# Layer 1 attention on TensorE: sixteen units written out instead of a loop, and another order of the work in front of the first step

## The reference

```python
q, k, v = (proj(wq), proj(wk), proj(wv))
q, k = apply_rope(q, k, sin, cos)
att = jnp.einsum('bhqd,bhkd->bhqk', q, k) * (1.0 / math.sqrt(HD))
att = jax.nn.softmax(att, axis=-1)
y = jnp.einsum('bhqk,bhkd->bhqd', att, v)
```

## Time and profile before

| | us |
|---|---|
| median of 3 runs | 3000.16 (2997.89 to 3001.02) |
| the profiled execution | 2999.55 |
| its span, first to last instruction | 2997.8 |
| first projection of layer 1 attention on PE | 1177.80 |
| first scores of unit 0 | 1244.63 |
| first copy of y (tick 2, step 0) | 1289.28 |
| last copy of y (tick 17, step 8) | 2402.01 |

### The profile page before, as it was taken

The page is one execution under the profiler, slowest core; times in us unless marked ns, Lnnn a source line. Parts: engine busy times, 40 slices in busy tenths (PEclk is TensorE's granted clock), DMA queues, the critical chain, the costliest instruction groups (busy, mean ns, idle before and its releaser), DMA issues. The chain is left out here.

```text
span 2997.8 us, 54358 instructions
## 1 busy us (share of the span) xinstructions
PE 2848.9 (95%) x19392; PEld 2011.7 (67%) x19392; DVE 1857.0 (62%) x2721; ACT 1291.0 (43%) x2021; POOL 1416.7 (47%) x1003
## 2 busy tenths in 40 slices
PE   6999999799999997799999999999999789999999
PEld 5878787688888886455555555555555368888887
DVE  5656766577777764666666666666666744444444
ACT  3221111266666663355555555555555522222222
POOL 2003555122333222377777777777777732222222
PEclk9999999999999998799999999999999999999999
DMA  3221211122232224122222222222222332222221
GB/s 127 88 61 49 65 61 53 36 71 85 84 105 84 84 90 160 58 71 71 71 71 72 71 71 71 71 71 71 72 78 77 121 127 85 85 89 86 91 84 49
DMA packets 124567, 238.99 MB, mean 80 GB/s; under 512 B 13440, under 2 KB 48384, under 8 KB 124416
## 3 DMA queue, kind: packets, MB, share of 16 engines
q1 hardware_dynamic: 120896, 235.32, 23.2%
q10 hardware_dynamic: 3520, 1.46, 0.2%
HBM read 178.02 MB, written 58.72 MB: 79 GB/s over the span
## 5 line engine op out<-in xcount | busy, mean ns | idle before, releaser
L1330 DVE TENSOR_REDUCE l_attn_maxima<-l_attn_ps_max 128x2 f32<-128x1024 f32 x502 | 613.6, 1222 | 234.2 <-PE l_attn_ps_max L1455 230.2
L1301 POOL TENSOR_TENSOR l_attn_summed<-l_attn_summed,stage 128x1024 f32<-128x1024 f32 x248 | 586.0, 2397 | 52.9 <-ACT stage L1239 52.9
L1239 ACT ACTIVATE stage<-l_attn_ps_sc 128x1024 f32<-128x1024 f32 x512 | 497.8, 1029 | 157.3 <-PE l_attn_ps_sc L1443 136.0
L1301 POOL TENSOR_TENSOR l_attn_summed<-stage 128x1024 f32<-128x1024 f32 x124 | 293.4, 2388 | 240.1 <-ACT stage L1239 240.1
L1702 POOL TENSOR_TENSOR l_ffn_ht_lo<-stage,l_ffn_ht_hi 128x512 fp32r<-128x512 f32 x88 | 114.0, 1296 | 413.9 <-ACT l_ffn_ht_hi L1723 413.9
L62 PE MATMUL l_attn_ps_prep<-l_w_tile,l_x_tiles 128*128 (+1 forms) x1440 | 287.1, 348 | 6.3 <-DVE l_attn_qk_lo L1324 2.0
L62 PEld LDWEIGHTS l_attn_ps_prep<-l_w_tile,l_x_tiles 128*128 128x128 f32 x1440 | 248.9, 190 | 39.3 <-issue 29.4
L1465 PE MATMUL l_attn_ps_y<-stage,l_attn_v 128*32 128x512 f32 x2048 | 273.6, 606 | 1.1 <-ACT stage L1239 1.1
L71 PE MATMUL l_ffn_ps_fc<-l_w_tile 128*128 128x512 f32 x1024 | 268.1, 405 | 6.7 <-DVE l_w_tile L865 5.0
L71 PEld LDWEIGHTS l_ffn_ps_fc<-l_w_tile 128*128 128x128 f32 x1024 | 184.6, 190 | 41.7 <-issue 5.5
L71 PE MATMUL l_ffn_ps_out<-l_ffn_t_proj,l_ffn_ht_hi 128*128 128x512 f32 x512 | 206.9, 404 | 0.0
(11 more groups left out here) (270 smaller groups left out, 6328.6 us busy)
## 6 DMA issues: line engine op xcount, KB each, us to landing
l_x_tiles<-xt_chunks SPq DMA_DIRECT2D x160, 512.0 KB, 3.7
xt_chunks<-l_w_tile SPq DMA_DIRECT2D x32, 512.0 KB, 4.7
l_attn_xin<-in_x SPq DMA_DIRECT2D x32, 256.0 KB, 4.3
l_attn_piece<-in_w_fcT SPq DMA_DIRECT2D x16, 512.0 KB, 4.3
s<-l_attn_s_sb SPq DMA_DIRECT2D x32, 256.0 KB, 2.2
l_attn_piece<-in_w_projT SPq DMA_DIRECT2D x16, 512.0 KB, 3.9
l_ffn_xa<-in_x SPq DMA_DIRECT2D x32, 256.0 KB, 2.7
l_ffn_xb<-in_x SPq DMA_DIRECT2D x32, 256.0 KB, 2.9
```

Source lines behind the costliest of these rows:

```text
L1239: act.activation(probs[kt % RING][:, hs, :], ps_sc[:, hs, :], ACT.Exp, scale=ATT_SCALE).then_inc(exp_done, 1)
L1301: pool.tensor_tensor(total[:, hs, :], old[:, hs, :], probs[kt % RING][:, hs, :], ALU.add).then_inc(added, 1)
L1330: dve.tensor_reduce(maxima[b][:, j, PAIR * hp:PAIR * hp + PAIR, half:half + 1], pair, AX.X, ALU.max).then_inc(max_read, 1)
```

## The change

1. `ticks` with its loop is replaced, for layer 1 attention, by `every`, which writes all seventeen ticks out, on all five engines. All waits are then for constants.
2. Unit 0 gets a table of maxima of its own, `FIRST_MAXIMA`, in the order of the query blocks: maxima 0 to 15 are the first block's, and the reduction to negated maxima follows maximum 15.
3. All 26 early maxima go to two pairs of banks in turn. The turn of the first block's maxima stands behind the 26th and no longer between the 21st and the 22nd.
4. The projections stand further ahead among the maxima, and projection (1,3) moves from the prologue to step 8 of tick 1, where the transpose (1,1) was; that goes to step 10, which was empty in tick 1. ScalarE's copies follow.
5. `maxes` and the order of the passes have a branch for three maxima in a step of tick 1; its surplus `more` is 16 + 10 - 26 = 0.

```diff
+        FIRST_EVENTS = {8: ("proj", 1, 3), 10: ("turn", 1, 1)}
...
+        FIRST_MAXIMA = [(j, hp, half) for qb in range(QB) for half in range(QB) for j in range(HALF * qb, HALF * qb + HALF) for hp in range(PAIR)]
...
-        FIRST_LATE, LAST_QB0 = 10, 19
-        TURNS_FOR = {0: 2, 8: 3, 12: 4}
+        FIRST_LATE, LAST_QB0, EARLY_MAXIMA = 10, 19, 26
+        TURNS_FOR, FIRST_TURNS_FOR = {0: 2, 8: 3, 12: 4}, {0: 2, 8: 4}
...
+            if isinstance(t, int) and t == 1:
+                more = 2 * CPB + FIRST_LATE - EARLY_MAXIMA
+                first = EARLY_MAXIMA + 2 * (s - CPB) + min(s - CPB, more)
+                return [(i // N_MAX, 1 - i // N_MAX, i % N_MAX) for i in range(first, first + 2 + (s - CPB < more))]
...
-            return ps_sc[:, 0:PAIR, :] if i <= LAST_QB0 and i % 2 == 0 else ps_max[:, :, :]
-
-        sched = (1, 2, NT, NT + 1)
+            return ps_sc[:, 0:PAIR, :] if i % 2 == 0 else ps_max[:, :, :]
+
+        def every(tick):
+
+            for t in range(1, NT + 2):
+                tick(t, t % 2)
...
-                        maximum(0, 0, i, early_pair(i), i if i > LAST_QB0 else i - 1)
+                        maximum(0, 0, i, early_pair(i), i - 1)
...
-                maxima_of(15, 18)
-                early_project(1, 3)
-                maxima_of(18, 21)
+                maxima_of(12, EARLY_MAXIMA)
                 need(pe, lo_ready, TURNS + 1)
                 turn_max(0, 0, turn_bank)
-                maxima_of(21, 26)
-                need(pe, proj_read, CPB + 4)
+                need(pe, proj_read, CPB + 3)
+                need(pe, max_read, EARLY_MAXIMA - 1)
...
-            ticks(pe, *sched, tick)
+            every(tick)
```

More of the change, by code:

```diff
@@ L1008, in layer1_attention @@
             EVENTS[2 * c + 1] = ("proj", 0, c)
+        FIRST_EVENTS = {8: ("proj", 1, 3), 10: ("turn", 1, 1)}
         def event(t, s):
+            if isinstance(t, int) and t == 1 and s in FIRST_EVENTS:
+                return FIRST_EVENTS[s]
             kind, back, i = EVENTS[s]
@@ L1020, in released @@
                 t, s = (t, s - 1) if s else (t - 1, STEPS - 1)
-                if isinstance(t, int) and t < 0:
-                    return None
+                if isinstance(t, int) and (t < 1 or t == 1 and s < CPB):
+                    return proj_read, CPB + 3
                 e = event(t, s)
@@ L1262, in _ @@
             prologue()
-            ticks(act, *sched, tick)
+            every(tick)
         @block.gpsimd
@@ L1303, in _ @@
             remainders()
-            ticks(pool, *sched, tick)
+            every(tick)
         @block.vector
@@ L1410, in tick @@
                         low(e[1], parity(p, EVENTS[s - 1][1]), e[2], ps_prep[:, :, :])
[L1411 removed]
+                    for a in todo[1:2]:
                         maximum(*a, ps_max[:, :, :])
@@ L1415, in tick @@
                         rope(e[1], e[2], ps_prep[:, :, :])
+                    for a in todo[2:]:
+                        maximum(*a, ps_max[:, :, :])
                     if isinstance(t, int) and t >= NT:
@@ L1423, in _ @@
             prologue()
-            ticks(dve, *sched, tick)
+            every(tick)
         @block.tensor
@@ L1447, in maximum @@
             def maximum(m, b, i, pair, read):
-                j, hp, half = MAXIMA[i]
-                if i in TURNS_FOR:
-                    need(pe, hi_ready, TURNS * m + TURNS_FOR[i])
+                j, hp, half = maximum_of(m, i)
+                turns = FIRST_TURNS_FOR if isinstance(m, int) and m == 0 else TURNS_FOR
+                if i in turns:
+                    need(pe, hi_ready, TURNS * m + turns[i])
                 need(pe, max_read, read)
@@ L1560, in tick @@
                     mine = (m, parity(p, 0 if s < CPB else 1), qb, kt)
-                    first, rest = ((0, 1), (2, 3)) if s % 2 else ((0,), (1, 2, 3))
+                    first, rest = ((0, 1, 2, 3), ()) if len(todo) > 2 else ((0, 1), (2, 3)) if s % 2 else ((0,), (1, 2, 3))
                     if live(m, NT):
@@ L1566, in tick @@
                         maximum(u, b, i, ps_max, N_MAX * u + i)
-                    if live(m, NT):
+                    if live(m, NT) and rest:
                         scores(*mine, rest)
@@ L1575, in tick @@
                         prepare(t, p, s)
+                    for u, b, i in todo[2:]:
+                        maximum(u, b, i, ps_max, N_MAX * u + i)
                 if isinstance(t, int) and t == 1:
```

46 lines of the change are left out of this document (21 added, 25 removed).

## The result

| | before | after |
|---|---|---|
| median, 4 runs each | 3000.59 us (2997.89 to 3002.36) | 2977.6 us (2975.44 to 2981.57) |
| ratio after to before | | 0.9922, 95% interval 0.991 to 0.9935 |
| profiled execution (span) | 2999.55 us (2997.8) | 2976.12 us (2974.4) |
| first projection of layer 1 attention | 1177.80 | 1177.44 |
| first scores of unit 0 | 1244.63 | 1233.86 |

Of the 23.4 us between the two spans, 12.8 are there at the first copy of y (0.4 of them at the first projection already), 10.1 come in the 28 half units of the loop, and the last 0.5 behind it.

What follows compares the result with a forecast made beforehand. PE was taken to bound the loop, DVE or its waits for half-clock projections the stretch ahead. -11.4 + 1.8 - 7.7 = -17.3 us from 2999.55, plus 0.6 for the median, gave 2982.9 us; range 2979 to 2991 us.

Steps and rivals of the forecast that it cites:

- part 2: Stretch ahead of the first step: two bank pairs and earlier projections bring first scores 11.4 us earlier (ends 12.9, 6.6).
- part 3: First half unit: projection (1,3) in step 8 and the transpose in step 10 add 1.8 us (ends +0.9, +3.2).
- part 1: Loop written out: its six jumps go, -7.7 us (ends -7.5, -8.7), with nothing more inside a step.
- Rival C: Loop: the jump's time isn't got back, other engines' catching up needs it; -9.6 us, 2990.6 us, chance 0.06.
- where I had reckoned 2.2: Step 8, half clock: projection (1,3) +4.17, transpose (1,1) -1.11, maximum 26 no longer waiting -0.89 us.
- where I had -1.0: Behind the first scores: slow clock lasts some 13 us again, the projection fills 2 us of it; -1.0 us.
- where I had +0.6: Step 10: the transpose moved out of step 8 comes again at full clock, +0.6 us.
- the 0.4 us at step 11: Half unit, upper end: unit 1's first maximum waits 0.4 us for ScalarE's copy of the transpose.
- the middle case: Ahead of first scores: projections (1,0), (1,1) keep the clock, (1,2) slow, DVE waits 1.5 us; scores 11.4 us earlier.
- B: Clock stays low through the whole stretch ahead of the first step: 6.6 us gained there, 2987.7 us, chance 0.14.
- D: First half unit: steps 8 to 15 bound by exponentials and sums, using up the front's gain; 2992.5 us, chance 0.08.
- E: Written-out loop: code loading stops PE, at 0.35 us per block slower, 3012.3 us; chance 0.06.

Runs made afterwards that it cites:

- e1: Kernel before with only the loop written out, on all five engines; 2990.83 us against 3000.43, ratio 0.9966.
- e3: Kernel before with the loop written out on PE alone; 1019.30 us for the 28 half units against 1027.83.
- f4: Changed kernel with two waits added on PE in step 8; first copy of y 45.59 us behind the first scores, 42.60 without.
- e2: Changed kernel with the loop of two units put back on all five engines; 2987.73 us, ratio 0.9954.
- e5: Kernel before with four units in the loop's body, three turns, two units written out behind; 1027.01 us for the 28 half units against 1027.83.
- f1: Kernel before with the loop written out and two pairs of banks for all early maxima; first copy of y 106.14 us from the first projection.
- f2: Kernel before with loop written out, projection (1,3) in step 8, transpose (1,1) in step 10; first copy of y 107.02 us from first projection.
- e7: Changed kernel with one pair of banks for maxima 20 to 25; first copy of y 103.89 us from the first projection against 99.02.
- e6: Changed kernel with projection (1,3) back in front, behind maximum 15, and transpose (1,1) back in step 8; 2977.96 us against 2999.57, ratio 0.9924.
- e4: Kernel before with the loop written out on the four engines other than PE; 1026.96 us for the 28 half units against 1027.83.

## Why the prediction was wrong

The direction was right, and so was what the change removes. Two terms of the sum were wrong: the loop's was too small, and the half unit's had the wrong sign. In the prediction's own steps, for the two profiled executions:

| step | predicted | measured |
|---|---|---|
| part 2, first scores | -11.4 | -10.4 (66.83 to 56.42) |
| part 3, half unit | +1.8 | -2.05 (44.65 to 42.60) |
| part 1, the loop | -7.7 | -10.1 (1027.83 to 1017.70) |
| sum | -17.3 | -22.6 |

The rest of the 23.4 us of the spans lies outside these steps: 0.4 ahead of the first projection and 0.4 behind the loop.

**Part 1** failed at the sentence "So nothing more is to be had inside a step". I compared steps 12 to 0 of a written-out tick with the same steps in the loop, and found 17.72 and 17.65 us. But the loop costs in step 1, which my comparison left out, and next to nowhere else: PE begins 0.30 us after the DVE work that it waits for instead of 0.05. It was to be seen beforehand in the half units themselves. 36.37 at the boundary inside the body is the half with steps 8 to 15; its neighbour in the same rows takes 36.49, and I took both for the same work. The list of PE's waits held the row as well (3.9 us, 14 times). e1 and e3 show 2.2 to 2.4 us for it. Why it costs there is argued, not shown by a run of its own: two register instructions stand between the signal and the matmul there, and where none does, a wait that reads a register costs no more than a constant one. The jumps themselves were sized rightly: 7.75 us over the six half units, 7.5 of it PE's idle time. That they are got back in full was luck in part, as e3 shows: with PE alone written out 1.6 us of them stay with the other engines, and it needs all five loops to go. Rival C had this mechanism, and for four units in a body it is the larger part.

**Part 3** failed at "The slow clock lasted some 13 us after the first scores before; if it does so again". It lasted 6. Step by step: step 8 took 0.7 us more than before (6.80 against 6.13), where I had reckoned 2.2, because the clock rose while projection (1,3) ran and it took 3.62 instead of 4.17 us, and because PE did the first passes faster without the waits. Step 9 took 2.9 us less (5.08 against 7.94), where I had -1.0, since it ran at 2.4 GHz throughout, and at 1.2 for its first 6.4 us before. The steps from there on took 0.1 more, where I had +0.6; the 0.4 us at step 11 that I kept as an end never came. What brings the clock back early is shown only in part. Idle time behind the first scores puts it off: f4 moved it from 5.6 (after; 5.3 in e2) to 9.3 by its two waits alone, and where the old step 8 has such waits (before, e1, e3 to e5, f1, f2) it is back after 9.3 to 12.3. But that isn't the whole of it: e7, with no idle time in step 8, and e6, with 0.17 us there, both have it back after 9.0 only. What decides between them and after stays open.

**Part 2** was 1.0 us too large. The choice of the middle case was right in kind: (1,0) and (1,1) fast, (1,2) slow. But DVE waited 2.48 us for (1,2), and 0.29 for the transpose ahead of it, not 1.5: the transpose (1,0) and the two pairs ahead were slow too, since the clock had fallen while PE waited 2.15 us for the read of maximum 8. e7 shows the better case, at about 2 us less.

The rivals: B (low clock throughout) didn't happen in any execution. The last train of maxima did run at 1.2 GHz, but DVE hid that. The rule of the Trainium skill that the prediction names (TensorE: Matmul & The Clock Gate, A second HAM failure mode: psum-queue depth-cycling) has the clock swing in work that cycles through banks; the trace agrees for the prologue, where it fell and rose again, and not for this train, where it stayed at 0.50 for 13 us. D didn't happen: the half unit gained. E didn't happen: the 28 half units without any loop average 36.35 us, and no idle time of type "issue" is left. In my range the run's spread had no room, and the two larger errors went the same way.

How much of the front's gain is the change's and how much the execution's? The same front code gave 111.5, 108.4, 111.5, 111.4 and 108.5 us in five executions of the old front (before, e1, e3, e4, e5), by the clock's course in the prologue, and 99.0 and 99.3 in two of the new (after, e2). So the front is worth 9 to 12.5 us, 11.1 in the mean; against the mean the prediction's 9.6 was 1.5 short, against the profiled pair 2.9.

## What to carry to other kernels

A loop of long units costs on each engine by itself: look for idle time of type "issue" at the jump on the bounding engine, and beyond it for waits whose start lags their signal: here PE began 0.25 us later than in written-out code at the one place of a unit where two register instructions stand between a wait's signal and the matmul. A longer body was no way out here (two jumps with four units cost 7.2 us, six with two 7.75); written out on all engines it is gone. Compare like with like when a comparison is to show that nothing else is there: whole units, not the part that is handy. And when an engine's queue starts a dense stretch at half clock, put work without waits first: in f4 two waits there cost their own 2.6 us, and the clock came back 3.7 us later, which cost 0.4 more.

## What the runs showed of the hardware

- PE began 0.30 us after the end of the DVE work it waited for at the projection of step 1 in the loop, where two register instructions stand behind the signal; 0.13 us in step 9, with one (1475.49 to 1475.62); 0.05 us in step 13, with none (1494.17 to 1494.22), and in written-out code.
- A jump back cost PE 1.00 to 1.42 us of idle time with two units in the body (before, e2, e4), 1.07 and 1.60 with four (e5); DVE 0.3 us at most with two units in its body, 3.59 and 2.71 with four, ScalarE 3.04 at the first jump with four.
- The instruction queue that serves the engines other than PE moved 5 packets during the loop of two units, none of them after its first turn, and 38 with four units in the body, four around each jump.
- With identical code the time from the first projection to the first copy of y was 108.4 to 108.5 or 111.4 to 111.5 us in five executions, by where the clock fell in the prologue.
- In after PE stayed at 1.2 GHz through the whole train of maxima, 13 us with 0.79 us of work in every 1.13; busy without a gap from the first scores on, it was back at 2.4 GHz 6 us later. In e7, just as busy from the first scores on, that took 9 us.
